# Three of the router's small operations move to the first pair of the second expert stage

## The reference, cut to what matters

```python
flat = _rmsnorm(x, ln2_w).reshape(-1, Cx)
probs = jax.nn.softmax(flat @ router_w.T, axis=-1)
tp, ti = jax.lax.top_k(probs, TOPK)                      # TOPK = 2 of NE = 8
tp = tp / (jnp.sum(tp, axis=-1, keepdims=True) + 1e-09)
weights = jnp.sum(tp[..., None] * jax.nn.one_hot(ti, NE, dtype=flat.dtype), axis=1)
out = jnp.zeros_like(flat)
for e in range(NE):
    hh = jax.nn.silu(flat @ w1[e].T) * (flat @ w3[e].T)
    out = out + weights[:, e:e + 1] * (hh @ w2[e].T)
return x + out.reshape(Bx, Tx, Cx)
```

## Time and profile before

| what | value |
|---|---|
| median of 3 runs | 1093.69 us (1091.11 to 1099.24) |
| profiled execution | 1098.7 us, its span 1096.8 us |
| PE busy | 1006.8 us, 92% of the span |
| DVE busy | 802.9 us, 73% |
| ACT busy | 579.9 us, 53% |
| POOL busy | 406.5 us, 37% |
| PE's granted clock over the span | 0.984 of full speed |
| second expert stage, tiles 0 to 12 | about 757 to 1079 us of the span |

### The profile page before, as it was taken

How to read it: one execution, slowest core, us unless ns; L and a number is a source line. 1 busy time by engine, 2 the same in 40 slices (tenths; PEclk the granted TensorE clock), 3 DMA queues, 4 the chain that set the end, 5 groups by cost and what they waited for, 6 DMA issues and landing times. The chain is left out here.

```text
span 1096.8 us, 23393 instructions
## 1 busy us (share of the span) xinstructions
PE 1006.8 (92%) x8389; PEld 723.9 (66%) x8389; DVE 802.9 (73%) x1969; ACT 579.9 (53%) x1331; POOL 406.5 (37%) x404
## 2 busy tenths in 40 slices
PE   5798989879999999998988789988999999999997
PEld 1376856567677767775765567765777777777774
DVE  2596858957776776677777589966877778777775
ACT  2275746565655556564337666765444444444441
POOL 3132902312433343333357568710133333333333
PEclk9899999999999999999999999999999999999999
DMA  8300000003223322322001000000122221211122
GB/s 221 142 2 1 3 2 1 1 14 86 49 51 76 71 50 50 83 65 50 1 19 50 7 2 2 2 3 0 51 65 69 73 65 55 56 55 56 56 56 67
DMA packets 76423, 50.16 MB, mean 46 GB/s; under 512 B 4196, under 2 KB 75124, under 8 KB 75924
## 3 DMA queue, kind: packets, MB, share of 16 engines
q1 hardware_dynamic: 75972, 44.59, 15.8%
q0 software_dynamic: 336, 4.07, 0.9%
HBM read 45.99 MB, written 2.66 MB: 44 GB/s over the span
## 5 line engine op out<-in xcount | busy, mean ns | idle before, releaser
L1576 PE MATMUL moe_psU<-moe_nT_parts,moe_w_hi 128*128 128x320 f32 x988 | 324.4, 340 | 12.4 <-DVE moe_hid L1480 7.6
L1576 PE MATMUL moe_psU<-moe_nT_parts,moe_w_lo 128*128 128x320 f32 x988 | 296.3, 310 | 0.0
L1576 PEld LDWEIGHTS moe_psU<-moe_nT_parts,moe_w_hi 128*128 128x128 f32 x988 | 187.4, 190 | 68.7 <-issue 41.8
L1222 ACT ACTIVATE moe_hid<-moe_psU,middle 128x320 f32<-128x320 f32 x312 | 149.6, 527 | 99.7 <-PE moe_psU L1576 98.1
L1217 ACT ACTIVATE moe_silu<-moe_psU 128x320 f32<-128x320 f32 x286 | 123.7, 438 | 139.9 <-PE moe_psU L1576 115.4
L1576 PEld LDWEIGHTS moe_psU<-moe_nT_parts,moe_w_lo 128*128 128x128 f32 x988 | 188.1, 190 | 0.7 <-issue 0.7
L1480 DVE TENSOR_TENSOR moe_hid<-moe_psU,moe_silu 128x320 f32<-128x320 f32 x286 | 131.3, 484 | 34.5 <-ACT moe_silu L1217 28.7
L1108 POOL TENSOR_TENSOR moe_y_sum<-moe_y_sum,moe_y 128x320 f32<-128x320 f32 x96 | 81.6, 871 | 145.4 <-DVE moe_y L1441 81.7
L1591 PE MATMUL moe_psY<-moe_hid,late 128*64 128x320 f32 x800 | 118.7, 439 | 0.0
L1591 PE MATMUL moe_psY<-moe_hid,middle 128*64 128x320 f32 x800 | 118.7, 439 | 0.0
L139 POOL TENSOR_TENSOR moe_stats<-moe_stats,minus_half 128x5 f32<-128x5 f32 x26 | 30.4, 1171 | 186.7 <-DVE moe_stats L1323 186.7
(11 more groups left out here) (367 smaller groups left out, 1904.2 us busy)
## 6 DMA issues: line engine op xcount, KB each, us to landing
moe_share<-shares SPq DMA_DIRECT2D x208, 160.0 KB, 4.4
images<-in_x SPq DMA_DIRECT2D x8, 576.0 KB, 11.5
late<-in_late POOLq DMA_DIRECT2D x1, 2263.5 KB, 11.3
out_tokens<-h SPq DMA_DIRECT2D x13, 160.0 KB, 1.8
middle<-in_middle POOLq DMA_DIRECT2D x1, 1554.0 KB, 6.9
project_turns<-in_turns SPq DMA_DIRECT2D x8, 160.0 KB, 2.2
early<-in_early SPq DMA_DIRECT2D x1, 1043.0 KB, 19.8
turns_first<-in_turns SPq DMA_DIRECT2D x4, 160.0 KB, 2.3
```

The source lines that it names most:

```text
L1222: act.activation(hid[hid_of(g, u)][:, :], psU[u % 4][:, 0:HALF], ACT.Relu, bias=late[:, c["b1"]][:, k:k + 1]).then_inc(hid_act, 1)
L1576: last = pe.matmul(psum[:, 0:HALF], w[:, col:col + SPLIT], moving, start=(part == 0), stop=(part == 1))
```

## The change

One line, the second expert stage's table of DVE's steps:

```diff
@@ -1083,7 +1083,7 @@
             TURN, KEEP = [(3, 1), (3, 3)], [(3, 1), (3, 3)]
             HI, EXP = (1, 3), (0, 3)
             NORM_STEPS, ASK_STEPS, END_STEPS = 2, 2, 18
-            SLOTS = {(0, 1): "aaaannn", (0, 4): "ee", (1, 1): "neeeeeee", (1, 4): "eee", (2, 1): "neeeeeee"}
+            SLOTS = {(0, 1): "aaaannnee", (0, 4): "eee", (1, 1): "neeeeeee", (1, 4): "eee", (2, 1): "neeee"}
```

## The result

The changed kernel takes 1088.27 us (median of 11 runs, 1081.81 to 1092.51) against 1096.91 us for the kernel before (11 runs, 1091.11 to 1099.86): a ratio of 0.9926, 95% interval 0.9905 to 0.9947, so 8.1 us less, between 5.8 and 10.4. A second comparison, made later beside two other versions, gave 0.9933 (0.9906 to 0.9959), 7.3 us less. The forecast was 7.2 us less, and 1086.5 us: it started from the median of three runs of the kernel before, 1093.69, and the median of all eleven is 3.2 us higher.

What follows compares the result with a forecast made beforehand. PE was taken to bound the kernel, busy 92% of the span and waiting on DVE evictions. Gains of 6.9 and 0.5 less 0.2 made 7.2 us, from the median 1093.69 to 1086.5 us; range 1081.5 to 1094.

Steps and rivals of the forecast that it cites:

- The place and the price: Unit 17's gate half on PE waits for DVE's late eviction of unit 14: 0.92 us in each of ten tiles.
- (0, 1) and (0, 4) are free: DVE operations moved to these two places in pair 0 cost PE nothing, through slack at unit 5 and idle DVE time.
- The thin cover: Slack of PE's unit 5 behind unit 2's eviction: 0.17 us, in truth 0.02; if it fails, one refill of 0.10.
- (1, 4) gives nothing: DVE leaves this place 0.4 us earlier, but the split then waits for POOL's L1108 and ends where it did.
- 0.69 per steady tile: Four operations instead of seven behind the split at (2, 1) bring unit 14's eviction forward: 0.69 us gained per steady tile.
- The rest of the sum: Ten steady tiles gain 6.9 us, the last tile 0.5, the first loses 0.2: 7.2 us in all.
- A new wait at unit 5: Sign of being wrong: PE newly waits at unit 5, where the slack was put at 0.17 us.
- handed on: PE is 0.7 us earlier at pair 3, but something fixed in time takes it back: 1093.7 us, chance 0.11.
- All comes back: Unit 14's eviction ends a tenth earlier than placed, so PE never stops there: 9.5 us gained, 1084.2 us, chance 0.14.
- L1419 misses the gap: At (1, 4) L1419 comes too late and may wait for L1108's first half: 0.3 us gained per tile, 1090.4, chance 0.10.
- The slower one: At (0, 1) POOL's power step L139 holds L1404, so PE waits 1.00 us at unit 5: 1098.6 us, chance 0.07.

## Why the prediction was right

- **The place and the price.** PE waits at unit 17 for unit 14's eviction, 0.92 us per tile in starts by the prediction. Taking DVE work away there, by one operation, by the split, by three operations and by more than that, gave 0.25, 0.42, 0.71 and 0.90 to 0.91; work moved at pair 0 alone gave 0.02. Of the 0.92, 0.10 was the routing's end at `turn_shares`.
- **(0, 1) and (0, 4) are free.** True in the steady tiles: two operations at (0, 1) alone gave 25.60, and five at (0, 4) gave the change's time. The thin cover I named at unit 5 held for two operations and was gone with three.
- **(1, 4) gives nothing.** The four lengths came as forecast: L1417 0.79, L1418 0.20, L1419 0.68 and the split 0.94 (forecast: about 1.0). DVE leaves (1, 4) 0.4 earlier and is held for as long at the split.
- **0.69 per steady tile.** Measured 0.70 to 0.71, and the 0.2 left over (forecast 0.12 and 0.10) stood where it was placed, at unit 17.
- **The rest of the sum.** Ten steady tiles gave 7.0 us in both profiles of the change (6.9 forecast). From L1347 in the last tile to the end of the span it is 39.6 us before and 39.1 after, the 0.5 that I took. For the first tile I took a loss of 0.2; the first two tiles together lost 0.05 in the repeated profile and 0.76 in the first one. So the profiles give 6.7 and 7.5 us for the forecast 7.2. The absolute 1086.5 says less: it lies 1.8 us below the measured 1088.27, and two medians of the changed kernel lie 2.0 apart.
- **Tile 1 of the first profile.** It took 24.86 instead of 24.16 us, because its first weighing waited 0.70 for the router's shares, which come through memory, and PE then waited for unit 2's eviction at unit 5 (the row at 777.48). A new wait at unit 5 was what I had named as a sign of being wrong; here the cause was not the slack that I had worked out:

```profile
776.20 0.82 DVE L1443 TENSOR_TENSOR moe_y<-moe_psY,moe_share 128x640 f32<-128x640 f32 x1 [0.70 <-DMA moe_share<-shares]
```

  In that profile SP could start its first load of the shares 3.6 us after their store, in the kernel before 1.3. The same kernel profiled again had 1.7 and lost nothing (24.17), so this is no fixed part of the change. In the first profile it is the rival "handed on" in one tile out of thirteen. Why SP waits 1.3 us behind the first tile's store in some executions and over 3 in others stays open; it was over 3 in four of the profiles, with three different tables.
- **The rivals.** "All comes back" needs one operation more, as the version with it shows. "L1419 misses the gap" did not happen, since the reduction was not held. The slower one, L1404 held by POOL's power step, had no occasion in the change, where L1404 began 0.17 ahead of the step in each of the twelve tiles that have one; and L1406, which stood inside the step in another version, was not held.

The rule of the Trainium skill (SBUF — State Buffer, Who interferes with whom) that the prediction names is borne out in two parts: a reduction beside a POOL addition takes its plain 0.20, and either engine can be the one that waits, DVE's split (1.08) or POOL's additions (2.02 against 1.68). For POOL's power step, which also reads SBUF, "the whole instruction" of that rule does not hold if it means the step's row in the profile: L1406 took 0.20 from 0.28 us into a row of 1.17. POOL's ends in the profile are rough, but its next operation also starts only 1.13 us after the step. The measurement decides.

## What to carry to other kernels

Where an engine's order is written out by hand, as DVE's is here, look for the pair of evictions around PE's marked wait and count from there: here small work was worth moving only out of the stretch between these two. Read PE's waits in starts of matmuls, not in marked idle time: 0.55 marked was 0.82, and a last 0.2 was not marked at all. Stop when the wait is gone: from there on an earlier DVE was worth nothing. Compare profiles from a row inside the stage that was changed, since 3.8 of the first 10.5 us lay ahead of it.

## What the runs showed of the hardware that was not expected

The engines of this kernel do not meet only at semaphores, as I wrote at the start: DVE and POOL also hold each other up where no semaphore stands between them. A DVE operation on 128x40 with two inputs in SBUF beside a POOL addition of 128x320 took 0.68 to 0.79 us instead of 0.2 (L1413, L1417, L1419). It is not a matter of two inputs alone: L1415, which reads one tensor, took 0.89 beside such an addition before, and 0.18 away from it after the change, while the reduction L1418 and the reciprocal L1416, with one input each, took their plain 0.20 and 0.40. Which engine waits depends on when each begins: DVE's split of 0.48, begun level with POOL's pair of additions, made them 2.02 us long instead of 1.68, and begun 0.12 us behind them it took 1.08 itself. POOL's power operation on 128x5, though 1.17 us long in the profile, did not hold a two-input DVE operation that began 0.28 us into it, in any of twelve tiles.
